# The up convolution with one matrix for both neighbour blocks, on a shifted copy of the image

## The reference

```python
x = x + _L0_conv_ref(_gn(x), bias, up_filter, dn_filter)  # repeat 2x2, 12x12 filter, leaky ReLU, 12x12 filter, every 2nd
t = _to_tokens(x)                                          # 16 x 1024 tokens x 32
t = t + _L1_attn_ref(_ln_t(t), Wq, Wk, Wv)                 # causal attention, one head, per image
t = t + _L1_ffn_ref(_ln_t(t), gate_w, gate_b, w1, w2)      # 16 experts, each takes its 8 best tokens per image
```

## Time and profile before

| what | us |
|---|---|
| median of three runs | 368.98 (368.06 to 369.28) |
| the profiled execution | 368.35 |
| its span, first to last instruction | 366.5 |
| TensorE busy | 327.2 (89%) |
| VectorE busy | 260.1 (71%) |
| ScalarE busy | 183.9 (50%) |
| GpSimd busy | 128.8 (35%) |
| mean granted clock of TensorE | 0.948 of full |

### The profile page before, as it was taken

The page is one execution under the profiler, slowest core; times in us unless marked ns, Lnnn a source line. Parts: engine busy times, 40 slices in busy tenths (PEclk is TensorE's granted clock), DMA queues, the critical chain, the costliest instruction groups (busy, mean ns, idle before and its releaser), DMA issues.

```text
span 366.5 us, 8381 instructions
## 1 busy us (share of the span) xinstructions
PE 327.2 (89%) x3362; PEld 249.3 (68%) x3362; DVE 260.1 (71%) x523; ACT 183.9 (50%) x251; POOL 128.8 (35%) x96
## 2 busy tenths in 40 slices
PE   2289998799999999999899999999996986979985
PEld 1168886587777878786678787777774544546774
DVE  2679779957757877869686876776988786454632
ACT  1043355446557574757663755576564547440500
POOL 6134535332444337554211557312235400351000
PEclk9999999999999999999999999999999899995655
DMA  4910100001011010101000101011021100100122
GB/s 125 204 36 3 26 19 16 16 16 31 16 18 26 5 32 2 31 4 32 15 16 2 31 15 17 17 16 26 7 58 32 31 2 18 28 2 29 57 75 69
DMA packets 35906, 11.16 MB, mean 30 GB/s; under 512 B 24431, under 2 KB 35741, under 8 KB 35869
## 3 DMA queue, kind: packets, MB, share of 16 engines
q1 hardware_dynamic: 33152, 9.98, 11.3%
q10 hardware_dynamic: 2717, 0.66, 1.2%
HBM read 5.72 MB, written 4.21 MB: 27 GB/s over the span
## 4 chain that ended last, share of the span: by engine, by line
PE 77%; DVE 10%; DMA 5%; issue 3%; ACT 2%; POOL 1%; ACTq 1%; SPq 0%; DVEq 0%; POOLq 0%
PE psB L892 14%; PE psA L892 13%; PE psB L1025 9%; PE psB L1005 8%; PE psA L990 7%; PE psA L1070 4%; PE psA L882 3%; PE psA L1048 3%; PE psB L1039 3%; DVE negmax L757 2%; PE psA L993 2%; PE psA L983 2%; PE psA L1032 2%; PE psB L1008 2%; PE psB L977 2%
## 5 line engine op out<-in xcount | busy, mean ns | idle before, releaser
L757 DVE TENSOR_REDUCE negmax<-psA 128x1 f32<-128x512 f32 (+7 forms) x128 | 90.5, 751 | 32.2 <-PE psA L993 31.6
L587 ACT ACTIVATE Pp<-psB 128x1024 f32<-128x1024 f32 (+1 forms) x80 | 73.6, 937 | 35.3 <-PE psB L1008 30.7
L892 PE MATMUL psB<-xin,UU 128*128 128x224 f16 (+1 forms) x480 | 56.4, 277 | 0.1
L892 PE MATMUL psA<-y,DD 128*128 128x224 f16 (+1 forms) x480 | 55.1, 273 | 0.0
L990 PE MATMUL psA<-zK,yQ 128*128 128x512 f16 (+1 forms) x192 | 47.8, 332 | 6.0 <-DVE uT L775 2.4
L892 PEld LDWEIGHTS psB<-xin,UU 128*128 128x128 f16 x480 | 47.0, 99 | 7.9 <-DVE xin L698 0.5
L1005 PE MATMUL psB<-yQ,zK 128*128 128x512 f16 (+1 forms) x192 | 47.3, 330 | 3.7 <-DMA yQ<-rows 2.4
L892 PEld LDWEIGHTS psA<-y,DD 128*128 128x128 f16 x480 | 46.7, 98 | 5.5
L477 POOL TENSOR_TENSOR zrstd<-zrstd,power 128x8 f32<-128x8 f32 x16 | 27.2, 1698 | 53.9 <-DVE zrstd L735 53.9
L557 ACT ACTIVATE y<-psB 128x1024 f16<-128x1024 f32 x16 | 16.4, 1023 | 44.8 <-PE psB L892 44.8
L499 POOL TENSOR_TENSOR y<-y 128x1024 f16<-128x1024 f32 x16 | 34.1, 2132 | 9.8 <-ACT y L560 9.8
(11 more groups left out here) (158 smaller groups left out, 504.5 us busy)
## 6 DMA issues: line engine op xcount, KB each, us to landing
x_all<-in_x_dram SPq DMA_DIRECT2D x4, 512.0 KB, 3.9
normalised_tokens<-z SPq DMA_DIRECT2D x16, 128.0 KB, 1.8
zV<-normalised_tokens SPq DMA_DIRECT2D x64, 32.0 KB, 2.1
out_dram<-x_all SPq DMA_DIRECT2D x8, 256.0 KB, 2.3
yQ<-rows SPq DMA_DIRECT2D x32, 2.0 KB
Pp<-filter_tables ACTq DMA_DIRECT2D x4, 121.9 KB, 3.7
w_halves<-y SPq DMA_DIRECT2D x12, 32.0 KB, 1.8
cst<-shape_constants SPq DMA_DIRECT2D x1, 326.5 KB, 4.3
```

The lines of the kernel that those rows point to most:

```text
L587: nc.scalar.activation(Pp[:, n % 2, UOFF[e[2]]:UOFF[e[2]] + N], slot(e)[:, 0:N], ACT.Exp).then_inc(b_drained, 1)
L757: ins = nc.vector.tensor_reduce(negmax[:, n % 2, m - 1:m], s[:, at:at + P * m], X, ALU.max, negate=True)
L892: ins = nc.tensor.matmul(within(out_cols, -shift), m, within(v, shift), start=i == 0, stop=i == len(matrices) - 1)
```

## The change

For output rows t = 1 and t = 2 the two neighbour matrices together use each partition only once: from the block after (k = +1) only the rows on partitions 0 to 63 are needed, from the block before (k = -1) only those on partitions 64 to 127. So the two become one matrix, if there is an image `mixed` whose partitions 0 to 63 hold the block after and whose partitions 64 to 127 hold the block before. The joint matrix is a place in `UU` into which the missing entries are also written (`filter_wrap`). For images 2 to 15 a row t = 1 or 2 then takes 2 x 3 products of 256 columns in place of 3 x 3, and an image 24 products in place of 30. Images 0 and 1 keep three matrices; there the products with the block after use 64 partitions for t = 1 and 2, since the others now hold the joint entries.

`mixed` has two homes. For each group SyncE makes it from `xin` with two DMA copies, each of 64 partitions and shifted by one number, once both pieces of the group's low part are written. The copy leaves wrong numbers in the columns at the edge of each plane; VectorE writes zeros there (event `edges`, two memsets). The first image of each group that uses `mixed` (2, 4, 8 and 12) waits for that event.

```diff
+PLAIN_UP = 2
-        group(6, "logit_exp"), batch(5, "up"), ...
+        group(6, "logit_exp"), *[once(GB * g - 5, "edges", g) for g in range(1, G)], once(PLAIN_UP - 5, "edges", 0), batch(5, "up"), ...
+        mixed = sb("mixed", [P, 2, 2, SLOT], F16)
+        def filter_wrap(r):
+            q, n = slice(C * r, C * r + C), r - 1
+            return (UU[q, :, SPAN - n:SPAN, :, :].rearrange("p i m q t -> p i (m q t)"),
+                    U_parts[q, :, 0:n, :, :].rearrange("p i m q t -> p i (m q t)"))
 # SyncE
+            for r in (R - 2, R - 1):
+                place_to, place_from = filter_wrap(r)
+                sp.dma_start(place_to, place_from).then_inc(UU_wrapped, 16)
+                elif name == "image_low":
+                    if g >= 2:
+                        sp.wait_ge(b_filled, BU["up", GB * (g - 1) - 1] + 1)
+                    sp.wait_ge(xin_ready, 2 * g + 2)
+                    first = BC * PLAIN_UP if g == 0 else 0
+                    v = xin[:, g % 2, :].bitcast(F16).rearrange("p (j n) -> p j n", j=2)
+                    sp.dma_start(mixed[0:2 * C, g % 2, :, first:SLOT - 1], v[0:2 * C, :, first + 1:SLOT]).then_inc(mixed_loaded[g % 2], 16)
+                    sp.dma_start(mixed[2 * C:P, g % 2, :, first + 1:SLOT], v[2 * C:P, :, first:SLOT - 1]).then_inc(mixed_loaded[g % 2], 16)
 # ScalarE, ahead of the first probabilities
+                        act.wait_ge(UU_wrapped, 16 * 2)
 # VectorE
+                elif name == "edges":
+                    dve.wait_ge(mixed_loaded[n % 2], 32 * (n // 2 + 1))
+                    first = BC * PLAIN_UP if n == 0 else 0
+                    nc.vector.memset(mixed[0:2 * C, n % 2, :, first + JW - 1:SLOT:JW], 0.0)
+                    nc.vector.memset(mixed[2 * C:P, n % 2, :, first:SLOT:JW], 0.0).then_inc(edges_zero, 1)
 # TensorE
+                    if n == PLAIN_UP or n > 0 and n % GB == 0:
+                        pe.wait_ge(UU_wrapped, 16 * 2)
+                        pe.wait_ge(edges_zero, n // GB + 1)
+                        if 1 <= t <= 2 and n >= PLAIN_UP:
+                            outer = [(UU[:, i, R - t + NS - 1, :, :], both[j], 0) for i, j in ((0, 0), (0, 1), (1, 0))]
+                        else:
+                            outer = [(UU[0:rows, i, R * k - t + NS - 1, :, :], parts[j][0:rows], k)
+                                     for k, rows in ((-1, P), (1, 2 * C if 1 <= t <= 2 else P)) if 0 <= R * k - t + NS - 1 < SPAN
+                                     for i, j in ((0, 0), (0, 1), (1, 0))]
```

More of the change, by code:

```diff
@@ L135 @@
         batch(0, "prob", 1), group(4, "proj", 1), batch(1, "score", 0), group(6, "select"),
-        group(6, "logit_exp"), batch(5, "up"), once(13, "w1", 0), group(7, "wT"), batch(0, "prob", 2),
+        group(6, "logit_exp"), *[once(GB * g - 5, "edges", g) for g in range(1, G)], once(PLAIN_UP - 5, "edges", 0), batch(5, "up"), once(13, "w1", 0), group(7, "wT"), batch(0, "prob", 2),
         once(2, "image", 2), once(6, "image", 3), once(1, "gn_var", 2), group(3, "mean", 0), once(18, "mean", 3, 1),
@@ L341, in hybrid_kernel @@
         U_ready = sem("U_ready")
-        UU_ready, UU_copied = sem("UU_ready"), sem("UU_copied")
+        UU_ready, UU_copied, UU_wrapped = sem("UU_ready"), sem("UU_copied"), sem("UU_wrapped")
+        mixed_loaded, edges_zero = [sem(f"mixed_loaded{i}") for i in range(2)], sem("edges_zero")
         sums_ready, U_split = sem("sums_ready"), sem("U_split")
@@ L952, in _ @@
                         pe.wait_ge(UU_copied, 2)
-                    parts = [v[:, BC * (n % GB):BC * (n % GB) + BC] for v in img[n // GB % 2]]
-                    for t in range(R):
+                    if n == PLAIN_UP or n > 0 and n % GB == 0:
+                        pe.wait_ge(UU_wrapped, 16 * 2)
+                        pe.wait_ge(edges_zero, n // GB + 1)
+                    of = slice(BC * (n % GB), BC * (n % GB) + BC)
+                    parts = [v[:, of] for v in img[n // GB % 2]]
+                    both = [mixed[:, n // GB % 2, j, of] for j in range(2)]
+                    for t in range(R):
+                        if 1 <= t <= 2 and n >= PLAIN_UP:
[4 more added lines that the diff above has]
+                                     for i, j in ((0, 0), (0, 1), (1, 0))]
                         ins = convolve(s[:, BC * t:BC * t + BC],
-                                       [(UU[:, i, R * k - t + NS - 1, :, :], parts[j], k) for k in (-1, 0, 1) if 0 <= R * k - t + NS - 1 < SPAN
-                                        for i, j in ((0, 0), (0, 1), (1, 0))])
+                                       [(UU[:, i, NS - 1 - t, :, :], parts[j], 0) for i, j in ((0, 0), (0, 1), (1, 0))] + outer)
                 elif name == "down":
```

## The result

| kernel | us, median | lowest to highest | against before |
|---|---|---|---|
| before | 368.52 | 367.83 to 369.28 (4 runs) | |
| after | 389.96 | 387.81 to 391.04 (4 runs) | 1.0574 [1.0515, 1.0633] |

The changed kernel is slower by 5.7%, where 375.0 us (369 to 380) was forecast: the direction is right, the size is not. The profiled execution of after took 387.81 us, its span 386.0, against 366.5 before.

What follows compares the result with a forecast made beforehand. The prediction took TensorE to bound the kernel, busy 89% of the span. Against the profiled 368.35 us it summed -8.67 (products), +12.21 (waits) and +2.6 (clock) to 374.5, stated as 375 on the runs' scale, range 369 to 380.

Steps and rivals of the forecast that it cites:

- products saved: Up convolutions of 14 images: six products fewer each at 0.1094 us, 0.656 us an image, 9.19 us in all.
- image 3's loss: At image 3 TensorE's next score needs VectorE's `yQ` write, so 0.52 of the 0.656 us saved is lost.
- I take 0.29 each: VectorE's edge memsets of 256 numbers: 0.29 us each, 0.58 a pair, from a cast of 0.294; image 2's 0.2 each.
- the upper bound of 0.43: Edge memsets: upper bound from a two-input operation on 256 numbers, 0.43 us, giving 0.9 a pair.
- I take 3.5 us: The pair of 256 KB copies for images 4 and 8: lands 3.5 us after the low part, between 3.0 and 5.7.
- copies that land later than 4.5 us after the low part: Sign in the changed kernel's profile: copies landing later than this would show the forecast wrong.
- 1.3 us for each of images 4 and 8 and nothing for 2 and 12: Clock falling behind the waits: 2.6 us in all; a 2.21 us wait before had met no fall.
- the clock did not hold: Rival on the clock behind the waits: the waits come but the clock holds, 372.5 us; chance 0.26.
- the loss at image 4: Image 4's wait, 4.78 us, was forecast to pass on; rival that it vanishes: 367.7 us, chance 0.13.
- the narrow products: Rival on the up convolutions: narrow products already cost less than wide ones, 2.3 us less gain, 377.4 us; chance 0.03.
- the slow copy: Rival at images 4 and 8: copies two bytes off take 5.7 us, waits 4.4 us longer, 379.5 us; chance 0.12.
- the four waits: TensorE waiting for VectorE's zeros at images 2, 4, 8 and 12: 1.97, 4.78, 3.32 and 2.14, together 12.21 us.

Runs made afterwards that it cites:

- hardly any zeros: The changed kernel with its eight memsets cut to one column each, other edge columns keeping what the copy put there: 378.67 us, 1.0256 of before.
- the waits filled: The changed kernel with TensorE computing 512-column products for nobody ahead of its waits at images 2, 4, 8 and 12: 382.39 us, 1.0372 of before.
- the bench: The kernel before with ten extra memsets at the start of VectorE's program and two on GpSimd's, on unused buffers; every 8th half-precision number: 1.14 us each.
- The two benches: The kernel before with extra memsets on unused buffers, then with five more pairs of other forms, one a multiplication by zero; no kernel time given.
- unshifted copies: The changed kernel with copies not shifted, so joint products compute something else: landings as in after, image 2's convolution 2.78 us; no kernel time given.
- twelve joint images: The kernel before with shifted copies, a separate joint table, joint form except images 0, 1, 4, 8, zeros where GpSimd was idle: 360.52 us, 0.979 of before.

## Why the prediction was wrong

How far the start of each up convolution moves from before to after gives a ledger (us; a wait counts with the 0.16 by which TensorE's products overlap without one):

| term | forecast | measured |
|---|---|---|
| products saved, less image 3's loss | -8.67 | -8.58: 0.66 an image; image 3 loses 0.61, as TensorE waits 0.45 behind it |
| wait at image 2 | 1.97 | 2.88 |
| wait at image 4 | 4.78 | 7.99 |
| wait at image 8 | 3.32 | 6.68 |
| wait at image 12 | 2.14 | 4.00 |
| clock behind the waits | 2.6 | 6.1 (1.58, 1.48, 1.39, 1.66) |
| image 1's products on 64 partitions | 0 | 0.41 |

The waits are 9.3 us over the forecast, the clock 3.5, image 1 0.4 and image 3 0.1: 13.3 us, and the profiled execution is 387.81 - 374.5 = 13.3 above the sum. (Image 1 starts 0.2 us sooner than before, and 0.2 are lost behind image 15; these cancel.) The median of the four runs lies 2.2 us higher still; no trace shows where. The start of the run may do it: in the kernels with hardly any zeros and with the waits filled, whose program is the same up to there, image 1 starts 2.1 and 1.0 us later.

1. **The step that failed most: "I take 0.29 each" for the memset.** A pair costs 2.46 us, not 0.58, image 2's 1.32 and not 0.40: 3 x 1.88 + 0.92 = 6.6 us of the 9.3 (2.46 is twice the pitch of 1.23 us; in the bench the pitch is 1.14). The nearest row was a cast to numbers side by side, the change writes every 8th; the upper bound of 0.43, from an operation on 256 such numbers, was no bound for this. The two benches and the kernel with hardly any zeros show it.
2. **"I take 3.5 us" for the pair of copies**: 4.7 at image 4 (64.53 + 4.03 - 63.84) and 4.9 at image 8, some 2.6 us of the 9.3. It lies inside the bounds (3.0 to 5.7), and nearer to their middle than to the table copies. That the copy is last at 4 and 8, and the maximum at 2 and 12, was right; the shift by two bytes plays no part. The forecast had named copies that land later than 4.5 us after the low part as a sign of being wrong, and this sign came.
3. **"1.3 us for each of images 4 and 8 and nothing for 2 and 12"**: the clock fell behind all four, and cost about 1.5 each. Images 2 and 12 were put at nothing because their waits were forecast at 2.0 and 2.1 us, as long as one that met no fall; they were 2.7 and 3.8. In the kernel with hardly any zeros their waits were 1.6 us and the clock held; so most of this error came out of the first step. But the 1.58 us of image 2 might as well have stayed out: with the same wait of 2.72 us the clock fell in two kernels and held in the one with unshifted copies.
4. **Image 1.** Its narrower products were not priced. It takes 3.86 us in after, and 3.44 where the joint filters have a table of their own and its products keep 128 partitions. The timeline of after:

```profile
28.84 3.86 PE L918 MATMUL psB<-xin,UU 128*128 128x256 f16 x30
```

The same row of the kernel with twelve joint images:

```profile
29.92 3.44 PE L936 MATMUL psB<-xin,UU 128*128 128x256 f16 x30
```

The rivals: the clock did not hold; the loss at image 4 passed on whole (image 4 starts 11.93 us later than before, image 5 12.79); the narrow products are not cheaper, the saving being 0.66 us an image; the slow copy came with 2.6 of its 4.4 us, and not for its reason. The range ended at 380; with copy and clock both at their upper bounds (16.6 us of waits, 6.8 of clock) the sum would have been 383.1, still below what was measured: the memset's bounds were false. That the kernel is slower was forecast for the right reason, the four waits.

What is left open: why a multiplication writes to the same places in half of a memset's time, and whether VectorE's memsets replaced by multiplications would save the changed kernel some of its waits; this was not tried. Nor is it known what decides whether the clock falls behind a wait of 2.7 us.

## What to carry to other kernels

A bound from the nearest row holds only for the same access pattern: ask how far apart the written numbers lie before you price a small write by its count. Work put on an in-order engine ahead of the bound engine's next step costs everything that stands ahead of it in that queue, and then the clock; put it where the trace shows that engine idle, as was done here for a gain of 7.8 us in place of a loss of 21.4. And leave out of the new form the units whose data come too late, here images 4 and 8.

## What the runs showed of the hardware

- A strided half-precision memset on VectorE shows 0.27 us but takes 1.14 for 256 numbers (every 8th), 0.57 (every 4th), 0.28 (every 2nd): the time is hidden ahead of its row. Look at the pitch, not at the length.
- Copies inside SBUF of 64 partitions landed after 1.8 us (0.2 KB), 2.5 (128 KB) and 3.8 (256 KB), shifted by two bytes or not.
- When the clock falls during a wait, a shorter wait can leave more of the low stretch to the products: convolutions of 4.18 us behind a wait of 6.52, of 5.08 behind 4.44 and of 5.28 behind 4.25. And the same wait of 2.72 us was followed by a fall in two kernels, and in one by none.
